# Key weights on ScalarE's queue, another order of the first tiles, and new orders for all engines in a fused cross-attention kernel

## The reference

```python
q = x @ Wq + bq                      # 1024 wide: 32 heads of 32
k = ctx @ Wk + bk                    # 256 wide: 8 heads of 32, shared by 4 query heads each
v = ctx @ Wv + bv                    # 256 wide
scores = q k^T / sqrt(32) + mask     # 512 x 512 per head
out = softmax(scores) v              # back to 512 x 1024
y = out @ Wo + bo + x
result = layernorm(y) * gamma + beta
```

## Time and profile before

| | |
|---|---|
| runs | 1725.77, 1730.63, 1730.64 us; median 1730.63 |
| profiled execution, its own time | 1726.1 us |
| its span, first to last instruction | 1724.1 us |
| PE (TensorE matmul) busy | 1603.3 us, 93% |
| DVE (VectorE) busy | 1449.9 us, 84% |
| ACT (ScalarE) busy | 1374.4 us, 80% |
| POOL (GpSimd) busy | 935.2 us, 54% |
| mean granted TensorE clock | 0.974 of full |
| DMA | 325.02 MB, mean 189 GB/s |

### The profile page before, as it was taken

How to read it: one execution, slowest core, us unless ns; L and a number is a source line. 1 busy time by engine, 2 the same in 40 slices (tenths; PEclk the granted TensorE clock), 3 DMA queues, 4 the chain that set the end, 5 groups by cost and what they waited for, 6 DMA issues and landing times.

```text
span 1724.1 us, 38438 instructions
## 1 busy us (share of the span) xinstructions
PE 1603.3 (93%) x14048; PEld 1110.3 (64%) x14048; DVE 1449.9 (84%) x2773; ACT 1374.4 (80%) x3186; POOL 935.2 (54%) x731
## 2 busy tenths in 40 slices
PE   4899889999999999999999999999989999999986
PEld 3565556676667666677566666667666676667654
DVE  4489889888788998889888898889988799788886
ACT  4588778778887788868988789887898778887884
POOL 5436344445754457534765457553585545955383
PEclk9899999999999999999999999999999999999998
DMA  9669987666875678667697577864877656876232
GB/s 186 184 161 227 236 233 204 183 157 178 239 220 157 156 189 278 182 166 161 189 284 185 147 175 207 258 182 122 206 230 240 166 139 169 280 229 166 69 97 104
DMA packets 357293, 325.02 MB, mean 189 GB/s; under 512 B 145777, under 2 KB 248177, under 8 KB 357105
## 3 DMA queue, kind: packets, MB, share of 16 engines
q1 hardware_dynamic: 354480, 322.55, 69.9%
q10 hardware_dynamic: 2624, 0.01, 0.1%
HBM read 244.85 MB, written 83.89 MB: 191 GB/s over the span
## 4 chain that ended last, share of the span: by engine, by line
PE 69%; DVE 17%; ACT 6%; issue 5%; POOL 1%; SPq 1%; DMA 0%; DVEq 0%; ACTq 0%; POOLq 0%
PE bank L1848 37%; PE bank L1928 16%; PE bank L1908 9%; DVE turned_p L1746 9%; DVE probs L1733 6%; PE bank L1943 2%; ACT probs L1632 2%; PE bank L1885 2%; PE bank L1968 1%; PE bank L1956 1%; ACT ring_hi L1601 1%; POOL ring_lo L1540 1%; SPq L1356 1%; ACT w_sb L1589 1%; DVE o_sb L1765 0%
## 5 line engine op out<-in xcount | busy, mean ns | idle before, releaser
L1848 PE MATMUL bank<-ring_hi,w_sb 128*128 128x512 f32 x2368 | 796.9, 400 | 33.0 <-POOL ring_lo L1540 15.8
L1632 ACT ACTIVATE probs<-probs,shift 128x512 f32<-128x512 f32 x1024 | 728.6, 715 | 62.1 <-DVE shift L1733 61.6
L1733 DVE CUSTOM_DVE_ANT_0 probs<-bank,mask_l 128x512 f32<-128x512 f32 x1024 | 650.9, 678 | 103.9 <-PE bank L1908 92.7
L1746 DVE STREAM_TRANSPOSE turned_p<-probs 128x2048 f32<-128x2048 f32 x256 | 588.1, 2302 | 100.8 <-PE bank L1928 79.9
L1528 POOL TENSOR_TENSOR w_sb<-w_raw,w_sb 128x512 fp32r<-128x512 f32 x320 | 412.1, 1295 | 332.5 <-ACT w_sb L1589 332.4
L1848 PEld LDWEIGHTS bank<-ring_hi,w_sb 128*128 128x128 f32 x2368 | 447.9, 190 | 156.5 <-issue 40.7
L1848 PE MATMUL bank<-ring_lo,w_sb 128*128 128x512 f32 x1184 | 471.6, 398 | 0.0
L1908 PE MATMUL bank<-k_stack,q_stack 96*128 96x512 f32 x1024 | 358.1, 414 | 6.4 <-DVE shift L1733 4.6
L1928 PE MATMUL bank<-turned_p,v_all 32*32 32x512 f32 x8192 | 303.8, 625 | 42.1 <-DVE turned_p L1746 31.6
L1540 POOL TENSOR_TENSOR ring_lo<-x_t,ring_hi 128x512 fp32r<-128x512 f32 x168 | 215.7, 1290 | 196.8 <-ACT ring_hi L1601 195.3
L1908 PEld LDWEIGHTS bank<-k_stack,q_stack 96*128 96x128 f32 x1024 | 188.8, 191 | 131.1 <-issue 55.3
(11 more groups left out here) (75 smaller groups left out, 961.1 us busy)
## 6 DMA issues: line engine op xcount, KB each, us to landing
w_raw<-w_d SPq DMA_DIRECT2D x144, 256.0 KB, 3.3
q_stack<-q_hi_d SPq DMA_DIRECT2D x128, 256.0 KB, 4.4
w_raw<-in_L_xattn_Wo_dram SPq DMA_DIRECT2D x128, 256.0 KB, 3.3
q_hi_d<-part_hi SPq DMA_DIRECT2D x64, 256.0 KB, 3.2
q_lo_d<-part SPq DMA_DIRECT2D x64, 256.0 KB, 3.7
q_stack<-q_lo_d SPq DMA_DIRECT2D x64, 256.0 KB, 4.2
v_all<-v_d SPq DMA_DIRECT2D x256, 64.0 KB, 3.1
out_dram<-y_sb SPq DMA_DIRECT2D x32, 512.0 KB, 4.1
```

The costliest lines, as they stand in the source:

```text
L1632: nc.scalar.activation(probs[:, st % 2, h, :], probs[:, st % 2, h, :], ACT.Exp, scale=-1.0, bias=shift[:, g % 2, i:i + 1], accum_out=sums[ ...
L1733: nc.vector.tensor_tensor_reduce(out=probs[:, st % 2, h, :], in0=S_ps[h][:, :], in1=mask_l[:, st, :], scale=-1.0, scalar=HIGHEST, op0=ALU. ...
L1746: nc.vector.transpose(turned_p[:, :, :, st, :].rearrange("p j h c -> p h j c"), probs[:, st % 2, :, :].rearrange("p h (j c) -> p h j c", c ...
L1848: mm = nc.tensor.matmul(C[c][:, :], w_sb[:, n_w, (1, 0, 0)[third], d % 4, :], (hi, lo, hi)[third], start=(n == 0), stop=(n == 23))
```

## The change

Three parts.

1. The eight DMAs of kv0's weights (two halves of four) are issued on ScalarE's queue as its first instructions, ahead of the bias loads; SP skips them.
2. The order of the tiles in the prologue is kv0 kv1 Q0 kv3 kv2 where it was kv0 Q0 kv1 kv2 kv3. `v_no` counts the values in the new order in the prologue.
3. All numbers of PLACES and BASE are new. No step is added or taken away.

```diff
-BASE = {1: 256.32, 2: 463.56, 3: 671.62, 4: 879.00, 5: 1086.39, 6: 1293.78, 7: 1501.17}
+BASE = {1: 240.84, 2: 449.36, 3: 657.66, 4: 863.57, 5: 1069.49, 6: 1275.41, 7: 1481.33}
 PLACES = {
     "pro": {
-        "x_load C": (0, 0.451),
+        "x_load C": (-0.307, 8.462),
...
-        "x_lo C": (10.72, 12.01, 13.64, 14.576, 15.279, 18.197, 20.232, 20.709),
-        "x_load X": (10.946, 20.106),
+        "x_lo C": (10.080, 11.996, 13.025, 17.102, 18.684, 22.505, 23.801, 27.612),
+        "x_load X": (9.246, 21.095),
...
         "w_load kv": (
-            (0.997, 16.331),
-            (20.117, 24.795),
-            (26.473, 37.306),
-            (38.548, 42.846),
+            (8.000, 13.800),
+            (9.235, 15.435),
+            (41.791, 41.948),
+            (29.393, 30.586),
         ),
...
         "w_lo kv": (
-            (18.21, 24.536),
-            (36.131, 38.067),
-            (41.062, 42.293),
-            (46.991, 48.258),
-        ),
+            (-0.011, 9.005),
+            (30.096, 30.207),
+            (46.358, 48.691),
+            (39.133, 40.025),
+        ),
...
 WINDOWS = {
-    "pro": {-1: "kv0 Q0 kv1 kv2 kv3"},
+    "pro": {-1: "kv0 kv1 Q0 kv3 kv2"},
...
         def v_no(t, m):
-            return 2 * (t + 1) + m - 1
+            return 4 - m if t == -1 else 2 * (t + 1) + m - 1
...
                 i = weight_id(what, m)
+                if (t, what, m) == (-1, "kv", 0):
+                    return
...
         @block.scalar
         def _(act):
+            for half in range(2):
+                for r in range(4):
+                    rows = wk.rearrange("(r k p) c -> r p k c", r=4, p=32)[r, :, 4 * half:4 * (half + 1), 0:P]
+                    act.dma_start(w_raw[32 * r:32 * (r + 1), WEIGHT[-1, "kv", 0, half] % NW, 1, :, :], rows)\
+                      .then_inc(w_in[WEIGHT[-1, "kv", 0, half] % NW], 16)
```

More of the change, by code:

```diff
@@ L62 @@
         ),
         "w_load Q": (
-            (11.052, 23.368),
+            (26.155, 27.855),
         ),
         "w_hi Q": (
-            (29.578, 31.197),
+            (31.735, 32.510),
         ),
         "w_lo Q": (
-            (31.263, 33.281),
+            (30.909, 32.292),
         ),
[L72 to L77, removed]
+        "keep Q": (39.295,),
@@ L78 @@
+        "hi Q": (41.059,),
+        "lo Q": (43.574,),
+        "store Q": (43.940,),
+        "v_turn": (None, None, 57.154, 51.955),
+        "v_store": (None, None, 59.645, 51.537),
     },
@@ new lines @@
+        "stack": (53.019, 72.831, 82.783, 109.567, 121.839, 149.370, 172.076, 202.407),
+        "recip": (83.273, 106.154, 129.937, 152.126, 173.799, 203.126, 224.928, 249.864),
+        "spread": (77.511, 106.059, 129.994, 143.779, 177.739, 214.624, 231.698, 238.191),
+        "v_load": (73.406, 82.794, 90.565, 119.252, 142.623, 150.389, 202.429, 218.446),
+        "pv": (82.223, 105.235, 128.605, 154.924, 176.844, 205.369, 228.550, 250.142),
+        "sel": (96.724, 115.881, 136.753, 161.657, 186.998, 212.606, 233.265, 253.398),
@@ new lines @@
+        "stack": (-22.030, 4.020, 34.268, 44.411, 74.601, 103.237, 139.572, 153.608),
+        "recip": (32.642, 59.261, 68.870, 110.230, 132.272, 156.750, 185.332, 206.999),
+        "spread": (27.024, 55.135, 81.311, 115.003, 134.907, 169.873, 195.682, 214.699),
+        "v_load": (4.009, 22.762, 45.670, 71.429, 105.301, 140.348, 170.407, 174.119),
+        "pv": (29.290, 52.958, 83.809, 108.357, 130.461, 159.009, 187.759, 213.526),
+        "sel": (41.772, 59.389, 89.099, 117.378, 140.128, 167.922, 199.065, 225.734),
@@ L335 @@
-            (125.251, 136.127),
-            (142.102, 148.282),
+            (107.094, 113.601),
+            (111.249, 122.183),
+            (136.421, 140.359),
+            (140.348, 146.751),
         ),
         "w_hi kv": (
-            (117.354, 122.531),
-            (130.358, 130.652),
-            (138.025, 145.22),
-            (146.357, 155.801),
+            (118.415, 129.268),
+            (130.853, 139.246),
+            (140.369, 147.705),
+            (148.858, 150.832),
         ),
@@ L426 @@
+            (182.244, 188.543),
+            (197.657, 197.815),
+            (198.347, 211.339),
+        ),
[4 rows of a table added]
         "mm o": (
[8 rows of a table removed]
[8 rows of a table added]
         ),
         "w_load o": (
-            (20.196, 33.65),
-            (36.139, 29.476),
-            (46.651, 55.59),
-            (57.4, 60.959),
-            (67.018, 83.66),
-            (74.086, 89.238),
-            (92.63, 91.262),
-            (97.456, 98.05),
+            (34.257, 39.168),
+            (36.683, 45.681),
+            (50.310, 58.541),
+            (74.612, 74.623),
+            (76.311, 76.300),
+            (75.283, 90.396),
+            (90.630, 90.619),
+            (101.713, 101.702),
@@ L469 @@
-        "y_turn o": (69.791, 73.509, 96.258, 98.681, 102.28, 119.672, 125.421, 148.015),
-        "y_add o": (70.283, 72.353, 97, 97.38, 104.628, 121.226, 126.414, 148.015),
+            (52.105, 55.124),
+            (55.124, 65.502),
+            (69.588, 77.760),
+            (81.034, 81.322),
+            (96.662, 97.435),
+            (97.441, 101.755),
+            (104.047, 106.487),
+            (108.194, 116.121),
+        ),
+        "keep o": (66.632, 69.973, 77.836, 93.010, 97.858, 106.448, 121.002, 129.094),
@@ L483 @@
+        "z o": (161.961, 167.293, 172.524, 191.406),
+        "zmul o": (165.951, 170.797, 191.184, 203.135),
+        "zadd o": (166.667, 189.162, 196.763, 216.096),
+        "z_store o": (185.433, 189.069, 223.257, 223.318),
+        "root o": 153.323,
+        "rstd o": 164.504,
     },
@@ new lines @@
+        "stack": (-13.589, 1.791, 15.273, 57.316, 80.380, 99.787, 138.118, 154.920),
+        "recip": (27.536, 52.859, 83.935, 94.890, 128.848, 154.568, 191.587, 210.880),
+        "spread": (22.845, 63.295, 77.076, 109.309, 126.865, 146.915, 195.261, 210.433),
+        "v_load": (-8.872, 33.693, 55.309, 97.844, 82.708, 140.439, 150.597, 158.296),
+        "pv": (28.871, 50.614, 78.464, 109.877, 128.150, 161.258, 182.512, 212.685),
+        "sel": (38.419, 61.754, 86.880, 116.972, 138.668, 167.616, 190.734, 220.464),
@@ L566 @@
-            (124.238, 128.398),
-            (129.428, 145.744),
+            (103.295, 107.650),
+            (105.045, 112.169),
+            (138.118, 141.382),
+            (141.371, 141.660),
         ),
         "w_hi kv": (
-            (111.972, 124.734),
-            (129.416, 132.839),
-            (133.745, 142.664),
-            (151.48, 153.757),
+            (121.145, 124.532),
+            (127.617, 135.176),
+            (143.533, 149.905),
+            (150.054, 150.685),
         ),
@@ L700 @@
-        "y_turn o": (70, 74.441, 92.369, 94.719, 101.746, 121.757, 126.962, 146.376),
-        "y_add o": (67.487, 74.702, 93.067, 95.375, 100.477, 121.2, 123.948, 148.698),
+            (44.605, 57.783),
+            (67.140, 67.140),
+            (73.540, 75.425),
+            (78.173, 78.653),
+            (81.852, 87.135),
+            (92.344, 92.344),
+            (104.420, 105.839),
+            (112.376, 112.983),
+        ),
+        "keep o": (62.751, 72.295, 74.890, 94.133, 100.577, 103.081, 122.139, 124.864),
@@ L714 @@
+        "z o": (175.192, 177.632, 182.852, 190.158),
+        "zmul o": (177.818, 191.458, 194.535, 206.791),
+        "zadd o": (179.786, 191.931, 204.841, 212.143),
+        "z_store o": (180.196, 195.011, 206.892, 210.102),
+        "root o": 157.025,
+        "rstd o": 165.515,
     },
@@ L775 @@
-        "mask": (-14.971, -9.848, -9.859, 2.447),
[14 rows of a table removed]
-        ),
[2 rows of a table removed]
+            (32.973, 33.394, 34.394, 34.608),
+            (53.340, 54.292, 57.356, 57.668),
+            (81.418, 81.975, 83.554, 89.270),
+            (108.034, 108.217, 108.860, 109.369),
+            (131.924, 132.827, 133.118, 133.595),
+            (159.137, 159.765, 160.158, 160.193),
+            (180.748, 183.824, 183.824, 184.222),
+            (204.355, 204.405, 202.871, 208.932),
+        ),
+        "stack": (-10.898, 4.952, 8.405, 46.540, 66.854, 77.379, 113.440, 125.868),
@@ L927 @@
-        "z_store e": (219.389, 226.507, 239.112, 241.941),
[2 rows of a table added]
+        ),
+        "res o": (7.053, 16.417, 29.690, 34.287),
+        "aggr o": (143.536, 148.475, 148.393, 150.138),
+        "z o": (156.612, 164.069, 166.822, 174.484),
+        "zmul o": (159.128, 167.787, 170.525, 173.458),
+        "zadd o": (161.164, 171.943, 185.646, 194.034),
+        "z_store o": (179.116, 184.684, 191.596, 206.143),
+        "root o": 150.380,
+        "rstd o": 153.698,
+        "res e": (-38.148, -16.994, 60.350, 60.570),
```

627 lines of the change are left out of this document (280 added, 347 removed), and 550 rows, old and new, of the table PLACES.

## The result

The kernel after took 1715.91 us (median of five, 1711.81 to 1718.09), the kernel before 1730.64 (1725.77 to 1736.86): a ratio of 0.9906, with a 95% interval of 0.9878 to 0.9935. The forecast was 1717.5. So the change is worth some 12 to 15 us. Two executions at a much lower granted clock, 1999.7 us of e1_start_only and 1832.36 us of the kernel before, stand in no ratio.

What follows compares the result with a forecast made beforehand. Middle batches were taken as bound by PE, batch 0 as hanging on VectorE. Terms -0.8 - 3.7 - 4.0 - 4.5 = -13.0 us took 1726.1 to 1713.1; 4.5 for the median gave 1717.6, stated as 1717.5, range 1706 to 1731.

Steps and rivals of the forecast that it cites:

- Part 1: Prologue: early weights and kv1 second put PE 4.2 us ahead at its end; context's first transpose 2.6 to 3.9 us later.
- Part 2: First score of batch 0: its stack load issued at 52.8 instead of 53.6, so -0.8 us, bounds -4.2 and +2.6.
- Part 3: Group 0 to group 1: five scores ahead of `pv` shrink VectorE's 7.55 us idle, -3.7 us, bounds 0 and -7.55.
- Part 4: Rest of batch 0: shorter VectorE waits for `pv` and less tile work on PE, -4 us, bounds 0 and -11.4.
- Part 5: Batches 1 to 7: more scores ahead of `pv`, -4.5 us (-1.0 batch 1, -0.6 each in five, -0.5 batch 7).
- B: Rival, 16%: new orders fit batch 0 and change nothing where PE is 97% busy; 1725 us.
- C: Rival, 12%: at the start the context's lost DMA time makes the first score 2.6 us later; 1729.5 us.
- D: Rival, 10%: `load_stack` 6 comes too late in each middle batch and PE waits; slower than before, 1742 us at 4 us each.

Runs made afterwards that it cites:

- e1_start_only: Kernel before with the new start (weights on ScalarE's queue, tile order, prologue table), old tables of batches 0 to 7: 1731.49 us, 0.9997.
- e4: Kernel after with the four bias loads moved on ScalarE's queue to ahead of kv1's first high part: 1726.04 us, 0.9973 of before.
- e6: Kernel after with kv1's matmuls, and the steps on their result, moved behind Q0's: 1731.80 us, 1.0016 of before.
- e7: Kernel after with kv0's eight weight DMAs on SP's queue as its very first, ahead of both context halves: 1716.65 us, 0.9926 of before.
- e2: Kernel before with its own start and the new tables of batches 0 to 7, moved 4 us later: 1725.77 us, 0.9973.
- e5: Kernel after once more, unaltered: 1717.88 us, 0.9926 of before.
- e8: Kernel before with the new start and the old tables of batches 0 to 7, run again for its trace: 1731.59 us.
- e9: Kernel after with the old table for batch 0 only, later BASE shifted to fit: 1725.11 us, 0.9969 of before.
- e10: Kernel before with the new start and the new table of batch 7, old tables of batches 0 to 6: 1728.39 us, 0.9999.
- e11: Kernel after with group 0's stack load directly behind Q0's store and its first seven scores ahead of most of q2: 1716.08 us, 0.9926 of before.
- e3: Kernel after with kv0's eight weight DMAs back on SP's queue at the new table's places: 1731.13 us, 0.9997 of before.

## Why the prediction was right, step by step

The total was forecast 13.0 us below before's profiled execution and 13.1 below the median; measured were 14.3, and 14.7 and 11.6 by the medians. Of its steps some held and some did not: the total came out partly by luck, since the gain was made in other batches than the sum had it.

**Part 1, the start: the sum held, the way there did not.** Tile work of the prologue ended at 53.3 as forecast, and Q0 at 42.3. But the first matmul came at 17.3, not near 14. I had ScalarE's issues "ahead of steps that wait for the context anyway" and priced them at nothing. They held the engine until 11.4, and the second half of the weights was there only at 13.1; by e4 the four bias loads account for 0.85 us of the delay. The context's first four DMAs lost only 0.6 us (first transpose 10.16), not the 2.6 to 3.9 of the sum, but the last of its eight landed at 17.2 where it was 15.4 before, 1.8 us later. There was hardly unused DMA time to draw on: from 4 to 9.6 us the DMA share is 1.29 before and 1.24 after. It carried more bytes in after, 188 GB/s from 6 to 9.6 us against 159, and fewer from 12 to 20 us, 174 against 194. Why is open. kv0 ended at 27.8 and kv1 ran 29.3 to 35.4, both 2 to 3 us late, and hidden, because Q0 is paced by its pieces of `x`. e6 shows that kv1 has to stand there, e7 that the queue is not what counts.

**Part 2, the first score: -0.8 forecast, -0.2 measured.** `load_stack` 0 was issued at 53.62, as before, not at 52.8: the eight issues with q2's weights ended at 53.0, later than the 52.5 of the sum. That the 4.2 us of PE's lead would not reach the first score was right. It was spent on the 34 matmuls ahead of it, which ended at 61.0; the stack had landed 0.3 us earlier, so an earlier load alone would have won nothing.

**Part 3, group 0 to group 1: -3.7 forecast, -3.1 measured** (+0.3 after group 0, -2.8 after group 1, and -3.1 as well in e2, on another start). The wait of 7.55 us gave way to one of 4.08 before `turn`, just past the 1.2 to 3.8 I wrote. The step missed a dependency: five scores stand ahead of `pv`, and there are four banks. The fifth needs the first max of group 1, which VectorE does only after the last `turn` of group 0. So `pv` began at 82.6, not at 80.9 plus the shift. It ran 5.75 us instead of 7.03, at a granted clock of 0.75 instead of 0.60, and made up for most of that.

**Part 4, the rest of batch 0: the step that failed.** I forecast 4.0 us more. By group 3 it was 1.2 more (-4.0 in the table); then it was given back, and batch 0 ended at -0.8, +0.5 and +1.8 in three executions with this order and first score. By first scores it is plainer: batch 1's came at 247.4, 248.3 and 250.0 in these three and at 247.1 before. The prediction wanted it some 8 us earlier and had put down "if batch 1 starts as late as before" as a sign of being wrong. That sign came true: the gain is not made in batch 0. What the traces show in its place:

- New waits took the place of the old. Waits of VectorE from 165 to 252 us in the kernel after (total, times, longest), where before had 9.3 and 1.4 us on the two lines of PE alone:

```profile
DVE turned_p L1753 <- PE bank L1935: 5.4, 2, 3.1
DVE turned_p L1753 <- ACT probs L1639: 3.3, 3, 1.5
DVE x_t L1707 <- DMA x_raw<-in_x_dram: 2.5, 1, 2.5
DVE probs L1740 <- PE bank L1915: 2.3, 1, 2.3
```

  In all 13.5 us against 10.7. The waits for `pv` went down by 3.9 as I had argued; waits for ScalarE's exponentials and for a load of `x`, brought forward in VectorE's order, came up by 5.8.

- Before's one profiled execution ran at a higher clock here. From 200 to 252 us its granted clock was 0.93; in the seven profiles of the other kernels that reach this stretch with a first score near before's (after, e5, e7, e8, e9, e10, e11) it was 0.87 to 0.90. How much of the loss is the clock was not isolated. The kernels with the old order of batch 0 and the new start lose there as well: e8 goes from -1.2 to +2.1, e10 from +0.2 to +3.9. Against e8, e9 and e10 (+2.1, +1.3, +3.9 after group 7, mean +2.4) the new order (-0.8, +0.5, +1.8, mean +0.5) is worth about 2 us, hardly more than these executions differ among themselves.

**Part 5, the later batches: about right in the middle batches, too small in batch 1 and the last.** Batch 1 was forecast at -1.0; from group 7 of batch 0 to the end of batch 1 it gave -5.4, -3.8 and -4.3 in after, e5 and e7. Between the first scores of batches 1 and 2 PE was idle 10.5 us in after and 9.5 in e5 (before 12.6) and busy 195.9 and 199.0 us (before 200.0): so 2 to 3 us are waits gone, the rest is busy time, at a granted clock of 1.00 and 0.98 against 0.96. VectorE's waits for `pv` there fell from 11.4 us to 3.6 and 7.2. The five middle batches were forecast at -3.0 together and gave -5.2, -0.9 and -4.5. Batch 7 was forecast at -0.5 and gave -2.8, -1.3 and -1.1. I had let PE's 6.1 free us bound a middle batch and reasoned to batch 1 from there, although its own row left 9.4 us free. Part 4 was 6 to 9 us too optimistic; part 5, which measured -13.4, -6.0 and -9.9, was 1.5 to 9 us too cautious. That the two nearly cancel is luck, and is why the total came out; the medians (-14.7, -11.6) agree with the mean of the three ends (-9.3) once before's 4.5 us are added.

These differences hang on one execution of before. The profiles together are a firmer base. The table has the time from first score to first score, mean and range in us. New are the seven kernels whose tables for batches 0 to 7 are those of after, unaltered (after, e2 to e7); old are before, e8 and, where their tables are the old ones, e10 (batches 0 to 6) and e9 (batch 0). The forecast for batch 0 is that of parts 3 and 4 together.

| stretch | old tables | new tables | gain | forecast |
|---|---|---|---|---|
| batch 0 | 188.7 (185.9 to 190.3) | 187.3 (186.4 to 188.8) | 1.4 | 7.7 |
| batch 1 | 212.6 (212.2 to 213.0) | 207.5 (206.2 to 209.9) | 5.1 | 1.0 |
| batches 2 to 6 | 1030.5 (1029.4 to 1031.4) | 1028.5 (1025.9 to 1031.0) | 2.0 | 3.0 |
| batch 7 to the end | 235.9 (235.1 to 236.8) | 231.4 (230.1 to 232.0) | 4.5 | 0.5 |

Only in batch 1 and in the last stretch do the ranges lie apart: these two give 9.6 of the 13 us, where the forecast had 1.5.

**The rivals.** B (start and batch 0 are all, 1725) fell: by the table batch 1 and the last stretch carry most of the gain, and the start alone gives 0.9997 (e1). C (the DMA engines set the start) fell: the first score came no later. It holds in one respect: e7 shows that issuing from a second queue brings nothing of its own. D (the stack of group 6 late in each middle batch) fell: the waits from 875 to 1079 us in the kernel after list no wait of PE for a stack, and the period is 204.9 us (205.3 before).

**How a late first score travels.** With the new tables of batches 0 to 7 it reaches the end almost whole. Against the two medians of the change, +11.1 at the first score is +13 to +15 (e3), +9.4 is +8 to +10 (e4), +7.3 is +8 to +10 (e2), and +15.3 is +14 against the one beside it (e6). An earlier one is not passed on (e11, e8): the next load or wait takes it.

**What stays open.** Why executions of one kernel part after group 3 was not settled; clock and landings both differ. Which edit of batch 1's order gives its 4 to 5 us was not isolated: e9 shows only that it depends on the order of batch 0. The new middle tables were not tried on batches 0 and 1 of before, so it is not known whether they, or the state in which batch 1 leaves the engines, bring the gain of the last stretch.

No experiment beat the change by more than its interval; e7 (with kv0's weights issued on SP's queue) and e11 equal it.

## What to carry to other kernels

- Time won at the start of an in-order pipeline counts only where the first step that everything hangs on comes earlier, or where work moves ahead of it. Here the lead of PE was spent on 34 matmuls ahead of the first score, and only then did the new orders pay; retune start and orders together, and measure each alone to see it.
- Fill the stretch in which PE waits for one input with a tile of another that is already there, and count what that tile's buffers hold up if it stands later.
- When the first score of the next group is put ahead of the last product of this one, count the banks: the score past the last free bank turns it into a wait for the consumer.

## What the runs showed of the hardware that I had not expected

- Issuing a DMA is not of fixed cost. The four bias loads, a few KB in all, took 0.45, 0.63, 0.49 and 0.49 us to issue in before, where they came first, and 0.46, 1.38, 2.13 and 2.54 us in after, behind eight weight loads on the same queue and beside the context's. ScalarE did nothing else in that time; its first work moved from 2.91 to 11.42 us.
- A load of a few KB can take as long as the large ones beside it. The last bias load was issued from 27.2 to 27.7 in e4, and ScalarE, waiting for it, went on at 34.8.
- The first 0.5 MB of weights beside the context cost its first pieces 0.6 us in after and 2.7 in e7, where they were wholly ahead of it (9.61, 10.16, 12.31 for the first transpose). At the last of the context's eight DMAs the two are nearly level: it landed at 15.4 before, 17.2 in after, 17.9 in e7.
